# Eight-layer stack: the second feed-forward product in three float32r passes, the query minimum on GpSimd

## What is computed

```
for i in range(8):
    residual = x
    Q  = elu(x @ Wq[i] + bq[i]) + 1
    Kf = elu(x @ Wk[i] + bk[i]) + 1
    V  = x @ Wv[i] + bv[i]
    KV, sumK = sum over the sequence of Kf * V, and of Kf
    att = Q * KV / (Q * sumK + 1e-6)
    x = layer_norm(gelu(att @ Wo[i] + bo[i]) + residual)
    residual = x
    h = gelu(x @ W1[i] + b1[i])          # 128 -> 512
    h = gelu(h @ W2[i] + b2[i])          # 512 -> 128, the product that changes
    x = layer_norm(h + residual)
```

## Time and profile before

| | |
|---|---|
| median of 3 runs | 3349.62 us (3346.64 to 3351.68) |
| the profiled execution | 3358.28 us, span 3356.5 us |
| PE busy in the span | 2989.0 us (89%) |
| DVE busy | 2665.6 us (79%) |
| ACT busy | 2443.9 us (73%) |
| POOL busy | 843.9 us (25%) |
| the stack's first and last query product | begin at 867.5 and 3130.0 us |

### The profile page before, as it was taken

The page is one execution under the profiler, slowest core; times in us unless marked ns, Lnnn a source line. Parts: engine busy times, 40 slices in busy tenths (PEclk is TensorE's granted clock), DMA queues, the critical chain, the costliest instruction groups (busy, mean ns, idle before and its releaser), DMA issues. The chain is left out here.

```text
span 3356.5 us, 51221 instructions
## 1 busy us (share of the span) xinstructions
PE 2989.0 (89%) x14363; PEld 1985.1 (59%) x14368; DVE 2665.6 (79%) x10483; ACT 2443.9 (73%) x4542; POOL 843.9 (25%) x1000
## 2 busy tenths in 40 slices
PE   6999998172599999999999999999999999999767
PEld 5777776161456666666666666666666666666444
DVE  4656665753489999988999999899999999898647
ACT  5888886031478888888888888788888888888643
POOL 2444444283111121111112112112111211121126
PEclk9999998586699999999999999999999999999868
DMA  1000000222100000000000000000000000000000
GB/s 54 1 0 0 0 0 14 100 34 38 64 1 1 20 13 1 20 7 8 1 25 8 1 20 7 8 12 15 7 1 20 13 1 1 1 1 1 1 7 26
DMA packets 31563, 46.34 MB, mean 14 GB/s; under 512 B 5315, under 2 KB 21731, under 8 KB 31334
## 3 DMA queue, kind: packets, MB, share of 16 engines
q1 hardware_dynamic: 25702, 39.46, 3.5%
q0 software_dynamic: 5632, 4.20, 0.9%
HBM read 35.16 MB, written 8.49 MB: 13 GB/s over the span
## 5 line engine op out<-in xcount | busy, mean ns | idle before, releaser
L1774 DVE TENSOR_SCALAR t_feat_q<-t_recip,t_neg_mean 128x256 f32<-128x256 f32 x1024 | 400.8, 453 | 112.4 <-ACT t_recip L1634 109.4
L1480 PE MATMUL t_o_ps<-t_feat_q,t_wo 128*128 128x512 f32 x1024 | 474.5, 596 | 6.8 <-issue 4.1
L1626 ACT ACTIVATE t_recip<-t_feat_q,t_z_scale 128x256 f32<-128x256 f32 x1024 | 434.8, 499 | 1.7 <-DVE t_feat_q L1774 1.0
L1612 ACT ACTIVATE t_exp_k<-t_k_ps 128x1024 f32<-128x1024 f32 x256 | 259.8, 1015 | 233.4 <-PE t_k_ps L1457 233.4
L1737 DVE CUSTOM_DVE_ANT_0 t_junk<-t_v_ps,t_feat_k 128x256 f32<-128x256 f32 x1024 | 390.7, 419 | 8.2 <-PE t_v_ps L1457 8.0
L1727 DVE SCALAR_TENSOR_TENSOR t_feat_k<-t_exp_k,t_k_ps 128x256 f32<-128x256 f32 x1024 | 369.4, 417 | 21.4 <-ACT t_exp_k L1612 21.4
L1898 POOL TENSOR_TENSOR t_var_eps<-t_moments,t_ln_eps 128x4 f32<-128x4 f32 x128 | 69.3, 542 | 1240.2 <-DVE t_moments L1785 1240.2
L1616 ACT ACTIVATE t_exp_q<-t_q_ps 128x1024 f32<-128x1024 f32 x256 | 261.7, 1022 | 87.1 <-PE t_q_ps L1457 86.3
L1763 DVE SCALAR_TENSOR_TENSOR t_feat_q<-t_exp_q,t_q_ps 128x1024 f32<-128x1024 f32 x256 | 312.7, 1222 | 8.8
L1480 PEld LDWEIGHTS t_o_ps<-t_feat_q,t_wo 128*128 128x128 f32 x1024 | 194.5, 190 | 180.9 <-issue 160.0
L243 POOL TENSOR_TENSOR a_probs<-a_probs,a_inv 128x256 f32<-128x256 f32 (+1 forms) x256 | 209.3, 839 | 274.5 <-DVE a_inv L340 274.5
(11 more groups left out here) (370 smaller groups left out, 7424.5 us busy)
## 6 DMA issues: line engine op xcount, KB each, us to landing
t_raw_w<-in_wk SPq DMA_DIRECT2D x8, 512.0 KB, 3.7
t_raw_w<-in_wq SPq DMA_DIRECT2D x8, 512.0 KB, 4.6
t_raw_w<-in_wv SPq DMA_DIRECT2D x8, 512.0 KB, 5.4
t_raw_o<-in_wo SPq DMA_DIRECT2D x8, 512.0 KB, 3.7
t_raw<-in_w SPq DMA_DIRECT2D x16, 256.0 KB, 2.7
x<-in_x SPq DMA_DIRECT2D x4, 512.0 KB, 6.9
tokens_dram<-r_hn SPq DMA_DIRECT2D x8, 256.0 KB, 2.3
e_w_raw<-in_fc_w SPq DMA_DIRECT2D x4, 512.0 KB, 3.8
```

The costliest lines, as they stand in the source:

```text
L1480: last = pe.matmul(o_ps[:], wo[:, chunk, :], feat_q[:, s, chunk, :], start=(chunk == 0), stop=(chunk == NC - 1), skip_group_check=True)
L1612: act.activation(exp_k[:], k_ps[:], ACT.Exp, bias=-1.0).then_inc(c["k_exp"], 1)
L1626: last = act.activation(recip[:, q % 2, k * UNIT + n * SEQ:k * UNIT + (n + 1) * SEQ], feat_q[:, s, chunk, cols], ACT.Ln, bias=1.0, scale=z ...
L1774: last = dve.tensor_scalar(feat_q[:, s, chunk, cols], recip[:, q % 2, k * UNIT + n * SEQ:k * UNIT + (n + 1) * SEQ], -1.0, neg_mean[:, s, n ...
```

## The change

The second product takes three float32r passes: `w2` is kept as a high and a low part (POOL makes both), and so is the GELU output. ACT copies `hid` to the float32r tile `hid_hi` in two halves of 128x1024, and DVE subtracts to get `hid_lo`, also in two halves. `min(exp_q, 1) - 1` goes from DVE to POOL (`less_one`), behind a one-column instruction (`carry`). DVE's `attention` becomes one `scalar_tensor_tensor` of 128x1024 for each quarter, with `neg_mean` spread along the tokens. For room, `g["x"]` is stored to HBM in the entry phase and holds the staging tiles and `hid` during the stack; half of it is loaded again at the end of the stack's list of transfers, half at the start of the finish. The diff, cut (declarations, semaphores and renamed arguments are left out):

```diff
 stack_entry_phase
+        @block.sync
+        def _(sp):
+            sp.dma_start(g["x_dram"], g["x"][:]).then_inc(x_stored, 16)
+            sp.wait_ge(x_stored, 16)
 stack_phase
-        raw_o = sb("t_raw_o", [P, NC, D])
+        raw_o = g["x"][:, 0:8, :]
...
-        hid = sb("t_hid", [P, NF, UNIT])
+        hid = g["x"][:, 16:32, :].rearrange("p (j a) d -> p j (a d)", j=NF)
+        hid_hi = sb("t_hid_hi", [P, NF, UNIT], F32R)
+        hid_lo = sb("t_hid_lo", [P, NF, UNIT], F32R)
 SP, behind its loop over the layers
+            sp.wait_ge(c["w2_ready"], LAYERS + 1)
+            sp.dma_start(g["x"][:, 0:16, :], g["x_dram"][:, 0:16, :]).then_inc(c["x_in"], 16)
 PE
             def second_feed_forward(u, follows):
-                pe.wait_ge(c["hid_ready"], 4 * u + 5)
+                pe.wait_ge(c["hid_hi_ready"], 2 * u + 3)
+                pe.wait_ge(c["hid_split"], 2 * u + 2)
...
-                    last = pe.matmul(m0[:], w2[:, j, :], hid[:, j, :], start=(j == 0), stop=(j == NF - 1))
+                    pe.matmul(m0[:], w2_hi[:, j, :], hid_hi[:, j, :], start=(j == 0), stop=False, skip_group_check=True)
+                    pe.matmul(m0[:], w2_lo[:, j, :], hid_hi[:, j, :], start=False, stop=False, skip_group_check=True)
+                for j in range(NF):
+                    if j == 2:
+                        pe.wait_ge(c["hid_split"], 2 * u + 3)
+                    last = pe.matmul(m0[:], w2_hi[:, j, :], hid_lo[:, j, :], start=False, stop=(j == NF - 1), skip_group_check=True)
 ACT
+            def split_hid(u, h):
+
+                act.wait_ge(c["hid_ready"], 4 * u + 2 * h + 3)
+                if h == 0 and (not isinstance(u, int) or u >= 1):
+                    act.wait_ge(c["w2_filled"], u + 1)
+                act.activation(hid_hi[:, 2 * h:2 * h + 2, :], hid[:, 2 * h:2 * h + 2, :], ACT.Copy).then_inc(c["hid_hi_ready"], 1)
 DVE
             def feature_q(t, s, q):
-                dve.wait_ge(c["q_exp"], 4 * t + q + 2)
-                dve.tensor_scalar(exp_q[:], exp_q[:], 1.0, -1.0, ALU.min, ALU.add).then_inc(c["q_less_one"], 1)
                 dve.wait_ge(c["q_less_one"], 4 * t + q + 2)
...
-                        last = dve.tensor_scalar(feat_q[:, s, chunk, cols], recip[:, q % 2, k * UNIT + n * SEQ:k * UNIT + (n + 1) * SEQ],
-                                                 -1.0, neg_mean[:, s, n, chunk:chunk + 1], ALU.add, ALU.mult)
-                last.then_inc(c["att_ready"], 1)
+                means = neg_mean[:, s, 2 * q:2 * q + 2, :].rearrange("p c n -> p (c n)").unsqueeze(2).broadcast_to([P, 4, SEQ])
+                dve.scalar_tensor_tensor(feat_q[:, s, 2 * q:2 * q + 2, :].rearrange("p c (n t) -> p (c n) t", n=2),
+                                         recip[:, q % 2, :].rearrange("p (a t) -> p a t", t=SEQ), -1.0, means,
+                                         ALU.add, ALU.mult).then_inc(c["att_ready"], 1)
+            def split_hid(u, h):
+
+                dve.wait_ge(c["hid_hi_ready"], 2 * u + h + 2)
+                dve.tensor_tensor(hid_lo[:, 2 * h:2 * h + 2, :], hid[:, 2 * h:2 * h + 2, :],
+                                  hid_hi[:, 2 * h:2 * h + 2, :].bitcast(F32), ALU.subtract).then_inc(c["hid_split"], 1)
 DVE's step: split_hid(t - 3, 0) behind feature_q(t, s, 1); split_hid(t - 3, 1) ahead of feature_q(t, s, 2)
 POOL
-                copy(w2[:], raw_2[:]).then_inc(c["w2_ready"], 1)
+                copy(w2_hi[:], raw_2).then_inc(c["w2_hi_ready"], 1)
+                pool.wait_ge(c["w2_hi_ready"], layer + 2)
+                pool.tensor_tensor(w2_lo[:], raw_2, w2_hi[:].bitcast(F32), ALU.subtract).then_inc(c["w2_ready"], 1)
+            def less_one(t, q):
+
+                pool.wait_ge(c["q_exp"], 4 * t + q + 2)
+                carry(3)
+                pool.tensor_scalar(exp_q[:], exp_q[:], 1.0, -1.0, ALU.min, ALU.add).then_inc(c["q_less_one"], 1)
 finish_phase
+            sp.dma_start(g["x"][:, 16:32, :], g["x_dram"][:, 16:32, :]).then_inc(c["x_in"], 16)
             sp.dma_start(w_raw[:], d["w_mix"]).then_inc(c["w_in"], 16)
 DVE, join(n)
+                if GT * n == TILES // 2:
+                    dve.wait_ge(c["x_in"], 16)
```

More of the change, by code:

```diff
@@ L1683, in step @@
                     exp_queries(t, 2)
+                if Dn:
+                    split_hid(t - 3, 1)
                 if E:
@@ L1842, in step @@
                     feature_q(t, s, 1)
+                if Dn:
+                    split_hid(t - 3, 0)
                 if E:
@@ L1881, in swap_wo @@
                 carry(0)
-                copy(wo[:], raw_o[:]).then_inc(c["wo_ready"], 1)
+                copy(wo[:], raw_o).then_inc(c["wo_ready"], 1)
             def swap_w1(layer):
@@ L1886, in swap_w1 @@
                 carry(1)
-                copy(w1_hi[:], raw_1[:]).then_inc(c["w1_hi_ready"], 1)
+                copy(w1_hi[:], raw_1).then_inc(c["w1_hi_ready"], 1)
                 pool.wait_ge(c["w1_hi_ready"], layer + 2)
-                pool.tensor_tensor(w1_lo[:], raw_1[:], w1_hi[:].bitcast(F32), ALU.subtract).then_inc(c["w1_ready"], 1)
+                pool.tensor_tensor(w1_lo[:], raw_1, w1_hi[:].bitcast(F32), ALU.subtract).then_inc(c["w1_ready"], 1)
             def swap_w2(layer):
@@ L1909, in step @@
                 s, r = at % 2, 1 - at % 2
-                C, Dn, E = (active(at, k) for k in (2, 3, 4))
+                A, C, Dn, E = (active(at, k) for k in (0, 2, 3, 4))
                 if at == 0:
@@ L1918, in step @@
                     swap_wo(closing)
+                if A:
+                    less_one(t, 1)
                 if E:
                     rstd_of(t - 4, 1, c["stats2_ready"], c["var2_ready"], c["rstd2_ready"])
+                if A:
+                    less_one(t, 2)
                 if C:
                     rstd_of(t - 2, 0, c["stats1_ready"], c["var1_ready"], c["rstd1_ready"])
-                if active(at, 0) and at != UNITS - 1:
+                if A and at != UNITS - 1:
                     split_x(t + 1, r)
+                if A:
+                    less_one(t, 3)
             swap_wo(0)
@@ L1999, in finish_phase @@
         out_ps = [ps(f"f_out_ps{i}", [P, 2, 4, D]) for i in range(2)] + [turned]
-        names = ("w_in gate_in b_in b_zeroed made order_made b_step b_ready w_hi_ready w_split diag_ready gate_filled gate_copied "
+        names = ("x_in w_in gate_in b_in b_zeroed made order_made b_step b_ready w_hi_ready w_split diag_ready gate_filled gate_copied "
                  "scaled turned_back x_joined bn_done stats_ready var_ready rstd_ready xn_ready h_filled h_ready h_hi_ready h_split "
```

32 lines of the change are left out of this document (20 added, 12 removed), and 4 rows, old and new, of the table names.

## The result

| | median, us | lowest to highest | runs |
|---|---|---|---|
| before | 3348.13 | 3345.82 to 3351.68 | 4 |
| after | 3888.44 | 3885.15 to 3895.65 | 4 |

The changed kernel takes 1.162 times as long (95% interval 1.160 to 1.164), 540 us more. The prediction had 3417 us, with 3370 to 3465 as its range: the side is right, the size is wrong by a factor of eight. One execution of a later kernel (the split on POOL) ran in a slow state, 4859.46 us at a granted clock of 0.55, and is left out of that kernel's figures.

A forecast was written before the change was run, and what follows sets the result against it. PE, 97% busy, was taken as nearly full, with handovers to ACT and DVE setting its waits. Losses of 0.39 + 0.57 us over 61 steps plus 8.5 us made 67 us: 3417 us against 3349.62, range 3370 to 3465.

The forecast's parts named there:

- The minimum on POOL, a loss: Between quarter 3's exponential and the next biases: POOL's link takes 1.30 us in place of 0.73, losing 0.57 us a step.
- upper bound: POOL's minimum at the queries: at most 2.01 us, as the same form took beside DVE's two-input subtractions, 0.96 us more.
- the rival on collisions: At quarter 3's end, POOL's minimum takes 2.01 us beside DVE's two-input work: 1.92 us a step, 3475 us; chance 0.13.
- The second half of the same part: Query features of the other three quarters: DVE work in front covers POOL's minimum, so no loss is counted there.
- the copy ahead of the GELU: ACT's first copy, about 0.98 us, delays the GELU of parts 2 and 3; PE's transpose comes 0.9 us late.
- product, key feature: From quarter 2's biases to quarter 3's: PE's 0.9 us lateness shrinks to 0.39 through the shorter product and DVE's key-feature chain.
- ACT's copies: Two copies of 128x1024 around GELU and state: of 1.96 us, 1.11 fill idle time and 0.84 reach PE each step.
- DVE's subtractions and the minimum's move at 1.05 us: DVE's key-feature chain gains 0.70 and pays 1.16 us, leaving the step 0.39 late; the minimum on POOL adds 0.57.
- the rest: Start, seven layer changes, load before the finish and last three steps: 8.5 us in all outside the ordinary steps.
- the second product on PE, a gain: PE's second feed-forward product: thirteen float32r passes take 3.1 us in place of 3.77, saving 0.65 us a step.
- The first rival: Handovers are hidden and PE alone sets the pace: 0.65 us a step won, 3318 us; chance 0.07.
- Rule and row: DVE's two-SBUF-input attention: the shared-interface rule has it go on meeting POOL, 3475 us; the rows of the place give 3417.

The follow-up runs named there:

- the split on POOL: The changed kernel with the query minimum back on DVE and the GELU output's copies and subtractions all on POOL: 3438.80 us, ratio 1.026.
- the run with the forms: The kernel before plus eleven forms of a 128x1024 POOL instruction, twice each, ahead of the stack's first weights: 3401.17 us, one execution.
- the second run: The changed kernel with POOL's minimum-and-add replaced by a multiply-and-add of the same size in the same place: 3423.47 us, ratio 1.022.
- the run without the split: The changed kernel with the minimum on DVE, GELU writing the high half itself, no copies or subtractions, low half left out: 3335.48 us, ratio 0.996.
- The first run: The changed kernel with the query minimum back on DVE and all else as changed: 3430.43 us, ratio 1.024.

## Why the prediction was wrong, and where it was right

**The step that failed** is the price in "The minimum on POOL, a loss": "1.05 for the same form of 128x1024", and its upper bound of 2.01 us. The row is a TENSOR_SCALAR of the same shape on the same engine, but line 1877 multiplies and adds, and the change takes a minimum and adds. The name in the profile is the same for both; the operations stand only in the code. Measured, the new instruction takes 3.63 us and the old one 1.05 (the run with the forms), and trading one for the other in the same place is worth 465 us (the second run). The upper bound was a bound for collisions, not for another operation, so the rival on collisions did not reach it either. The trace before held no row of a minimum on POOL; the price and its upper bound both came from multiply-and-add.

The second half of the same part fell with it: "The other three quarters have DVE work in front of the feature, which covers it." At 1.05 us it does: in the second run DVE's rows show a wait for POOL, 0.87 us, before the feature of quarter 3 only. At 3.63 us DVE waits for POOL in quarters 0 and 1 as well (line 1802 is the attention):

```profile
2012.43 1.37 DVE L1802 SCALAR_TENSOR_TENSOR t_feat_q<-t_recip,t_neg_mean 128x1024 f32<-128x1024 f32 x1 [3.24 <-ACT t_recip L1663]
2015.35 1.22 DVE L1793 SCALAR_TENSOR_TENSOR t_feat_q<-t_exp_q,t_q_ps 128x1024 f32<-128x1024 f32 x1 [1.54 <-POOL t_exp_q L1946]
...
2028.09 1.22 DVE L1793 SCALAR_TENSOR_TENSOR t_feat_q<-t_exp_q,t_q_ps 128x1024 f32<-128x1024 f32 x1 [2.53 <-POOL t_exp_q L1946]
...
2048.89 1.22 DVE L1793 SCALAR_TENSOR_TENSOR t_feat_q<-t_exp_q,t_q_ps 128x1024 f32<-128x1024 f32 x1 [3.62 <-POOL t_exp_q L1946]
```

**The steps that held** show in the second run, which is the changed kernel at the price that the prediction took. Two rows of before, from the same timeline as the earlier trace rows, give the pieces:

```profile
2007.89 0.39 PE L1450 MATMUL t_k_ps<-t_ones_b,t_b 3*128 3x512 bf16 x2
...
2017.02 0.39 PE L1450 MATMUL t_k_ps<-t_ones_b,t_b 3*128 3x512 bf16 x2
```

| from the biases of quarter | before | with multiply-and-add | difference | predicted | after |
|---|---|---|---|---|---|
| 0 to 1 | 9.56 | 9.56 | 0 | 0 | 11.82 |
| 1 to 2 (the copy ahead of the GELU) | 9.13 | 10.09 | +0.96 | +0.9 | 10.54 |
| 2 to 3 (product, key feature) | 9.90 | 9.39 | -0.51 | 0.39 - 0.9 = -0.51 | 11.08 |
| 3 to 0 (the minimum on POOL) | 6.59 | 7.14 | +0.55 | +0.57 | 9.72 |
| step, us | 35.18 | 36.18 | +1.00 | +0.96 | 43.16 |

The transpose waits 0.91 us for the GELU, as foretold, and the second product 0.31 us for the state. The last column less the third is 6.98 us a step: 2.58 in the last piece, which is 3.63 less 1.05 in full, 1.69 and 0.45 where DVE, late by the feature of quarter 1, keeps PE waiting (PE's rows show 0.85 and 0.51 us for DVE's `t_y` in the third piece and the 0.27 above before the biases of quarter 2), and 2.26 in the first piece, most of it the clock (below). The step shown is like the others: over the 59 steps from the fifth on, the means are 35.57, 36.60 and 43.60 us, so 1.03 and 7.00 us apart.

**The terms, from the runs** (each against the run that differs from it by that part):

| part | predicted, us | measured, us |
|---|---|---|
| the product in float32r passes (measured: with the rest) | -40 | -13.5 |
| ACT's copies | +51 (0.84 x 61) | +58.2 |
| DVE's subtractions and the minimum's move at 1.05 us | +47 (0.20 + 0.57, x 61) | +35.6 - 7.0 = +28.6 |
| the rest | +8.5 | in the first row |
| minimum-and-add in place of multiply-and-add | 0 | +467 (540.3 - 73.4, each against its own before) |
| sum | 67 | 540 |

By the means of the steps, 4 us (the run without the split, -13.5 + 0.29 x 61) to 11 us (the second run, 73.4 - 1.03 x 61) are left for the rest. So "the second product on PE, a gain" was right by its passes and too high by its effect: the prediction's 0.65 us a step is there, but PE alone does not set the pace. Nor do the parts simply add: too much was given to the product's gain and too much to the loss by the subtractions and the move, and these errors cancel in part. That the sum without the last row comes so near (67 us predicted, 73.4 measured) is in part luck, though the pieces of the step came out as foretold. The first rival's 3318 us was too good as well: without the copies, the subtractions and the move of the minimum the kernel still took 3335. The first run's own expectation was missed by another slip: it kept the 0.70 us that the removed minimum gives to DVE's chain, in a kernel that has the minimum there again. With those, 43 us in 61 steps, the 3381 us of its sum become 3424, against 3430 measured.

**Rule and row.** The Trainium skill (GPSIMD Engine Reference, section 1, Specifications) says that POOL contends with DVE instructions that have two SBUF inputs. The trace agrees where they meet: in the run with the split on POOL the attention took 2.75 us beside POOL's subtraction, 1.22 alone. But it is not what made this loss, for the minimum took 3.63 us with or without DVE at work: at 2011.69 with DVE's attention of two SBUF tensors beside it (2012.43), at 2045.23 with DVE waiting for it. The same page of the Trainium skill (section 4.1, Engine selection) calls one-input elementwise work on POOL roughly line rate. The runs do not bear out one rate: 1.05 us for multiply-and-add, but 3.63 us for minimum-and-add of the same shape, which DVE did in 0.69 us.

**What stays open.** Why POOL is fast with a multiplication in front of a second operation and slow otherwise is not known, and nothing was tried beyond these eleven forms; multiply-and-minimum, for one, is not among them. The 1.69 and 0.45 us of the middle pieces are read from the rows of one step; no run of their own confirms what makes them.

## What to carry to other kernels

A row of the trace is a price for a new instruction only if the operations agree too, not just the engine, the instruction's name and the tile; where no row has the operation, the range has no upper end from the trace, and a probe of one instruction is cheaper than the argument. Work taken off an engine that is 97% busy is worth only what the engine next in line lets through: here less than half of PE's saving came through while DVE's chain stayed (13.5 of 40 us), and most of it (82 of 96 us) once that chain was shorter. And of two free places for the same instruction on one engine, the one ahead of what others wait for can cost twice the one behind it (58 against 28 us here).
